# Expert order by place in the group, unpaced returned gathers and token-row gathers up to eight pairs ahead, in a macaron MoE and linear-attention block

## The reference

```python
logits = x @ gate_weight.T                      # 32 experts = 8 groups of 4
scores = softmax(logits)
group_scores = scores.reshape(T, 8, 4).max(axis=-1)
_, group_idx = top_k(group_scores, 3)           # 3 groups of 8
tmp_scores = where(expert is in one of these groups, scores, 0.0)
topk_weight, topk_idx = top_k(tmp_scores, 6)    # 6 experts of the 12
topk_weight = topk_weight / (topk_weight.sum() + 1e-20)
combine = zeros((T, E)).at[token, topk_idx].add(topk_weight)
for each expert e:
    y += combine[:, e] * ((silu(x @ w1[e].T) * (x @ w3[e].T)) @ w2[e].T)
y += (silu(x @ sw1.T) * (x @ sw3.T)) @ sw2.T    # the shared expert
```

## Time and profile before

| what | value |
|---|---|
| median of 3 runs | 855.51 us |
| the runs | 852.6, 855.51 and 856.67 us |
| span of the profiled execution, first to last instruction | 856.4 us |
| its own device time | not listed apart from the runs above |
| mean granted TensorE clock | 0.913 of full speed |
| layer 1, attention, layer 2 with its shared expert | about 0 to 296, 296 to 490, 490 to 856 us |
| loop of layer 2 | about 556 to 766 us |

### The profile page before, as it was taken

How to read it: one execution, slowest core, us unless ns; L and a number is a source line. 1 busy time by engine, 2 the same in 40 slices (tenths; PEclk the granted TensorE clock), 3 DMA queues, 4 the chain that set the end, 5 groups by cost and what they waited for, 6 DMA issues and landing times. The chain is left out here.

```text
span 856.4 us, 16278 instructions
## 1 busy us (share of the span) xinstructions
PE 734.5 (86%) x4554; PEld 590.7 (69%) x4555; DVE 515.1 (60%) x1439; ACT 361.0 (42%) x799; POOL 468.9 (55%) x487
## 2 busy tenths in 40 slices
PE   5888999999999987999999582799999999998900
PEld 5556788888888645777777481578888888874600
DVE  5685864444422568999997459977444442246652
ACT  2261444444455314556665231534444455531100
POOL 4003755555346455888864340275555637678784
PEclk9987999999999999999999755589999999999955
DMA  6792466744336552222232042144444435582234
GB/s 216 287 380 88 129 251 221 258 153 159 142 134 215 205 197 87 81 75 77 87 92 82 1 139 95 29 124 156 154 158 173 154 134 191 187 291 81 86 99 147
DMA packets 43591, 128.80 MB, mean 150 GB/s; under 512 B 8432, under 2 KB 16784, under 8 KB 40720
## 3 DMA queue, kind: packets, MB, share of 16 engines
q1 hardware_dynamic: 25104, 77.76, 24.1%
q0 software_dynamic: 18432, 50.36, 19.7%
HBM read 78.80 MB, written 49.28 MB: 150 GB/s over the span
## 5 line engine op out<-in xcount | busy, mean ns | idle before, releaser
L405 POOL DMA_INDIRECT back<-token_table,slots x192 | 186.2, 970 | 208.6 <-DVE slots L658 96.8
L930 PE MATMUL bank<-w,xt 128*128 x1024 | 244.7, 382 | 1.0 <-issue 0.6
L930 PEld LDWEIGHTS bank<-w,xt 128*128 128x128 f32 x1024 | 188.3, 192 | 24.7 <-issue 2.5
L706 DVE TENSOR_TENSOR mids<-mids,bank 128x256 f32<-128x256 f32 x128 | 53.7, 420 | 180.5 <-ACT mids L481 180.5
L950 PE MATMUL bank<-w,mids 128*128 x512 | 132.7, 382 | 0.1
L432 POOL DMA_INDIRECT back<-slot_table,combine x76 | 80.2, 1055 | 53.5 <-PE bank L930 25.1
L504 ACT COPY xt<-ring 128x256 f32 x256 | 91.2, 407 | 42.2 <-DVE ring L696 42.2
L950 PEld LDWEIGHTS bank<-w,mids 128*128 128x128 f32 x512 | 87.4, 190 | 9.1 <-issue 2.2
L481 ACT ACTIVATE mids<-bank 128x256 f32<-128x256 f32 x128 | 49.1, 384 | 102.3 <-PE bank L930 99.9
L696 DVE COPY ring<-bank 128x512 f32 (+1 forms) x96 | 66.3, 691 | 37.8 <-PE bank L920 37.0
L201 POOL DMA_INDIRECT ring<-slot_table,combine x64 | 65.4, 1021 | 27.1 <-issue 17.4
(11 more groups left out here) (208 smaller groups left out, 1096.5 us busy)
## 6 DMA issues: line engine op xcount, KB each, us to landing
slot_table<-gT SPq DMA_DIRECT2D x32, 512.0 KB
slot_table<-ey SPq DMA_DIRECT2D x32, 512.0 KB
w<-in_w SPq DMA_DIRECT2D x12, 1024.0 KB, 17.1
slot_table<-w SPq DMA_DIRECT2D x6, 1024.0 KB
token_table<-back SPq DMA_DIRECT2D x8, 512.0 KB, 2.9
back<-token_table,slots POOLq DMA_INDIRECT x192, 2.8
x<-in_x SPq DMA_DIRECT2D x4, 512.0 KB, 6.1
turn_a<-in_turn SPq DMA_DIRECT2D x4, 512.0 KB, 3.6
```

The costliest lines, as they stand in the source:

```text
L405: pool.indirect_dma_start(out=rows[q % RX][:, a * H:(a + 1) * H], out_offset=None, in_=table, in_offset=bass.IndirectOffsetOnAxis(ap=slots ...
L706: nc.vector.tensor_tensor(two(eg[u % 2][:, :]), two(es[u % 2][:, :]), part(u, 1), ALU.mult).then_inc(e_g, 1)
L930: last = nc.tensor.matmul(bH[u % 2][:, a * 2 * I:(a + 1) * 2 * I], xt[u % 2][:, a * H + k * P:a * H + (k + 1) * P], w13[:, bass.ds(expert[ ...
```

## The change

It has four parts. The columns of the mask, the exponentials and the weight arrays go by the place of an expert in its group: the first experts of the eight groups, then the second ones, and so on (`by_place` on the chip, `placed` on the host). The returned gathers of layer 2 no longer wait for `e_h`; those of layer 1 wait as before. The token-row gathers of layer 2 may be eight pairs ahead of the transposes, instead of four; layer 1 keeps four.

```diff
-AHEAD = 4
+AHEAD = 4, 8
-PACED = NQ - NT, NQ - 20
+PACED = NQ - NT
...
-                            if q >= AHEAD:
-                                pool.wait_ge(e_xp, read + q - AHEAD + 1)
+                            if q >= AHEAD[f]:
+                                pool.wait_ge(e_xp, read + q - AHEAD[f] + 1)
...
-                                if g % 2 == 0 and PACED[f] + g // 2 <= NQ:
-                                    pool.wait_ge(e_h, done + PACED[f] + g // 2)
+                                if f == 0 and g % 2 == 0 and PACED + g // 2 <= NQ:
+                                    pool.wait_ge(e_h, PACED + g // 2)
...
+                        def by_place(ap):
+
+                            return ap.rearrange("p (t e g) -> p t g e", g=NG, e=EG)
...
-                        nc.vector.tensor_scalar(v3(msk16[:, :], E), v3(val_out, PADE)[:, :, 0:E], 3e38, None, ALU.is_equal
-                                                ).then_inc(s_chosen, 1)
+                        nc.vector.tensor_scalar(by_place(msk16[:, :]), v3(val_out, PADE)[:, :, 0:E].rearrange(
+                            "p t (g e) -> p t g e", e=EG), 3e38, None, ALU.is_equal).then_inc(s_chosen, 1)
...
-                        nc.vector.tensor_tensor(v3(equal[:, :], E), v3(lg, E), wide(red[:, :], E), ALU.subtract
-                                                ).then_inc(s_d, 1)
+                        nc.vector.tensor_tensor(by_place(equal[:, :]), by_group(lg), red[:, :].unsqueeze(2).unsqueeze(3)
+                                                .broadcast_to([P, NT, NG, EG]), ALU.subtract).then_inc(s_d, 1)
...
+    def placed(m):
+
+        return m.reshape(NG, EG, *m.shape[1:]).swapaxes(0, 1).reshape(m.shape)
+
-    w13 = np.stack([a["w1"], a["w3"]]).reshape(2, NG, EG, I, KC, P).transpose(5, 1, 2, 4, 0, 3)
+    w13 = np.stack([placed(a["w1"]), placed(a["w3"])]).reshape(2, NG, EG, I, KC, P).transpose(5, 1, 2, 4, 0, 3)
...
-        "w2": a["w2"].transpose(2, 0, 1).reshape(I, -1),
+        "w2": placed(a["w2"]).transpose(2, 0, 1).reshape(I, -1),
```

## The result

The changed kernel takes 854.78 us at the median of 20 runs, against 857.15 us for the kernel before in 20 runs of the same comparison. The ratio is 0.9972, with a 95% interval of 0.9959 to 0.9985: faster by 0.28%, and so within the 0.5% called no change above. Forecast were 850.5 us, 0.6% faster. The range held the time; the size of the step was wrong. Two of the 20 runs of the changed kernel took 1485.85 and 2088.17 us and are not in the ratio; without them its median is 854.66 us.

A forecast was written before the change was run, and what follows sets the result against it. The kernel's end was taken as g46's start, plus 50 gathers, plus what VectorE's runs of adds cost them. 856.4 - 3.8 (gathers) - 1.5 (loop's end) + 0.3 (mask) = 851.4, stated as 850.5 us; range 847.0 to 855.5.

The forecast's parts named there:

- The pace: Layer 2's returned gathers, no longer waiting for TensorE, start g46 with the first add; gain three gathers, 3.8 us.
- The three limits on the gathers: Layer 2, g0 to g45: stores allow g0 at 688.0, last token-row gather near 684.6, buffers; g45 near 753.
- the idle time of 10 us: GpSimd in layer 2, after g45 near 753: idle some 10 us until VectorE's first add frees a buffer.
- the one long gather in the first run: In VectorE's first run of adds behind layer 2's loop, g48 is held up and takes over 3 us.
- The loop's end: End of layer 2's loop: the store lands 2.6 us earlier, at 759.8, so ScalarE stops waiting; gain 1.5 us.
- The mask: Strided write of the mask (L582), on the path in each layer: costs 0 to 0.5 us, taken as 0.3.
- The sum: Whole kernel: 856.4 - 3.8 - 1.5 + 0.3 = 851.4; stated as 850.5 us, the median lying 0.9 below the span.
- the main case: Whole kernel: gathers, loop's end and mask as summed, 850.5 us, own range 849.0 to 852.3; chance 0.47.
- (b): First run of adds behind the loop lets gathers through, 2.2 us more gain: 848.3 us; chance 0.13.
- (a): Loop's end stays as it was, only the gathers gain: 852.0 us; chance 0.2.
- (c): Nothing gets through the first run of adds, unpaced gathers bring nothing, only the loop's end gains: 854.3 us; chance 0.12.
- (d): Slower: faster gathers hold up stores between 741 and 762 us; store landing at 771 gives 860 us; chance 0.08.

The follow-up runs named there:

- a3: Changed kernel with mask, exponentials and weights back in the old group-by-group order of experts; 852.82 us, ratio 0.9961 to the kernel before.
- c2: Kernel before with only the pace (wait for `e_h`) of layer 2's returned gathers taken away, old order and four pairs of lead; ratio 0.9956.
- c1: Changed kernel with the pace of 44 + g/2 put back for layer 2's returned gathers, new order and eight pairs of lead kept; ratio 1.0001.
- b1: a2 with `KEEP = 24`, so 42 buffers for returned rows instead of 46; ratio 0.9984 to the kernel before.
- c3: a2 with column 0 and half of column 1 added inside the loop, and the store of pairs 56 and 57 ahead of the four loads; 841.8 us, 0.9811.
- a1: Changed kernel run again unaltered; 853.15 us against 855.86 for the kernel before, ratio 0.9953.
- a4: Kernel before with the order of experts by place alone, paced and four pairs of lead; 856.16 us, ratio 0.9988.
- a2: Changed kernel with the mask and `equal` lines reading with the stride and writing in a row; ratio 0.9949 to the kernel before.

## Why the prediction was right or wrong

**The pace: right, in place and size.** Forecast were three gathers, 3.8 us. B without long gathers is 80.5 to 80.6 in the three paced profiles and 76.2 to 77.0 in the five unpaced ones with 46 buffers and whole adds behind the loop: 3.5 to 4.4. The three limits on the gathers (stores, GpSimd's own order, buffers), the idle time of 10 us and the one long gather in the first run stand in the profile as forecast. That order and lead give nothing at g46 is shown by a3 and c2, and from the other side by c1.

**The loop's end: right in mechanism, too large in size.** I took 1.5 us and counted the store as early enough; 0.9 was measured. It landed near 760.65 (751.17 + 9.48), in a loop that ran 0.73 us ahead of the one before; on the clock of the profile before that is 761.4, where 759.8 was worked out and 760.9 would have been early enough. A fell by 1.07 in this profile and, by the means of the two profiles of the changed kernel (3.6) and of the three paced ones (4.5), by 0.9. The step assumed that the queue of the loads and stores drains at the common rate once the gathers are gone. A follows when the gathers end: 2.82 when they end at 749 (b1), 3.3 to 4.0 at 753, 4.3 to 5.0 when they run on. Beside the loads that are queued ahead of the store (c3), the few gathers up to 753 still cost something, and the estimate gave them nothing.

**The mask: this is the step that failed.** The term was "between 0 and 0.5 us, and I take 0.3", bounded above by the row of L585. By the rows it is 0.86 us in each layer (1.28 to 1.31 against 0.43), 1.7 in all. In layer 2 the path shows it: from its first transposes to its first `up` it is 65.67 to 65.85 us in the four profiles with the strided write (changed, a1, a4, c1) and 64.85 to 64.98 in the three with the old one (before, a3, c2). In layer 1 it doesn't stand out: from the mask's start to the first `up` it is 46.7 to 49.1 us in those four and 48.2 to 48.3 in those three. The bound was no bound: I took a row with as many elements, but written in a row, as the price of a strided write, and L585 itself became slower under its stride, 1.06 against 0.69. No row of before showed a strided write of this kind. The Trainium skill (VectorE: DVE Perf Modes, section What auto-detection actually checks) gave 0 as I read it; the trace says otherwise, and the measurement decides. Reading with the stride costs 0.18 to 0.19 us (a2).

**The sum.** With the forecast's 3.8 for the pace, which its 3.5 to 4.4 holds, and with what was measured for the others it is -3.8 - 0.9 + 1.7 = -3.0 us, -0.35%. The measured ratio is 0.9972 (0.9959 to 0.9985), a1 has 0.9953 (0.9932 to 0.9973), and -0.35% lies within both. The forecast was -5.0. Of the 4.3 us between 850.5 and 854.78, 1.6 are the median before (857.15 instead of 855.51), 1.4 the masks and 0.6 the loop's end; the remaining 0.7 is less than the runs spread. The same terms give 0.9956 for c2 (0.9956 measured), 0.9949 for a2 (0.9949), 0.9956 for a3 (0.9961) and 1.0020 for c1 (1.0001, with 1.0020 as the end of its interval). For a4 they give 1.0020 as well, and there they fail (0.9988, at most 1.0007). So the part of the masks rests on the rows and not on the times.

Two slips in the prediction's own figures changed no term. The bounds of the mask and the store (0 to 0.5 and 0 to 1.5) give the main case 850.2 to 852.2 us, and not 849.0 to 852.3, so less of it was below 851.2 than the two thirds that the chance of "faster" counts. And the profile before has a long gather in four of its five runs of adds, not three.

**The rivals.** (b) happened in a2, whose adds and gathers are those of the changed kernel. It is less a rival than a throw of each execution: of the nine profiles with all adds behind the loop and two SBUF operands (before, changed, a1 to a4, b1, c1, c2) the first run has a long gather in eight, the second in seven. One more or less is 1.9 to 3.9 us in these nine, as much as the whole change. (a) happened in part: the loop's end kept 0.6 of its 1.5 us. (c) and (d) did not happen. The time stands near the 854.3 us of (c), but by chance: two gathers got through the first run and the unpaced gathers did bring their 3.8 us. The store was never as late as (d) needs. That the range held the time is luck in part too, since most of the masks' cost and the higher median before were in none of its terms.

**What stays open.** Why one gather of a run of adds is held up until its end, and why in some executions none is, at the same distance from the run's start to 0.01 us. The other spread, ahead of layer 2, was not tested either. In layer 1 the granted clock fell at different times; the rows give busy times, granted clock, DMA share and GB/s, before and then after (columns: the stretch and its length, busy time and number of instructions of PE, PEld, DVE, ACT and POOL, then the clock, the DMA share and GB/s):

```profile
38.00:45.00 7.00, 2.43 (x32) 1.74 (x32) 6.48 (x31) 2.42 (x4) 0.00 (x0) 1.00 1.01 427
45.00:54.00 9.00, 8.85 (x18) 3.83 (x19) 7.31 (x31) 3.89 (x4) 0.00 (x0) 0.81 1.01 421
...
66.00:84.00 18.00, 14.09 (x65) 11.75 (x64) 11.84 (x48) 2.61 (x3) 6.24 (x7) 0.71 0.18 61
```

```profile
38.00:45.00 7.00, 4.45 (x33) 2.46 (x32) 6.48 (x28) 3.00 (x4) 0.00 (x0) 0.76 1.01 427
45.00:54.00 9.00, 8.12 (x25) 4.18 (x26) 8.04 (x32) 3.55 (x4) 0.00 (x0) 1.00 1.01 422
...
66.00:84.00 18.00, 14.09 (x74) 11.86 (x71) 12.66 (x50) 2.61 (x3) 7.88 (x8) 0.81 0.22 71
```

A clock of 1.00 is the level of 2.4 GHz, and the means between mix it with 1.2. Before, the clock was down in part of the stretch from 45 to 54 us, after in part of that from 38 to 45, and from 66 to 84 it was up for longer. The first `up` of layer 1 started at 87.25 before and 85.60 after although the mask came 0.8 us later, and in a1, the same kernel, it started at 87.16.

## What to carry to other kernels

When a later stage is bound by a queue of transfers, count how many of them are left when the first buffer comes free, and price the change in whole transfers: here 1.27 us each, checked by taking four buffers away. If buffers are the limit, free them earlier instead of filling them faster; the adds moved into the loop took the ratio to 0.979, where the kernels without the pace alone stand at 0.995 to 0.997. And price a reordering by a row with the same stride on the same side; here reading with the stride and writing in a row was the cheaper form.

## What the runs showed of the hardware that was not expected

- A write of 128x512 in float16 with a stride of 8 elements took VectorE 1.28 to 1.31 us from float32 in SBUF, against 0.43 us in a row and 0.61 to 0.62 us with the stride on the reading side. In float32 from PSUM it was 1.06 against 0.69 us, and 0.69 with the strided read.
- In runs of VectorE's adds with two SBUF operands a gather of GpSimd takes up to 8.01 us instead of 0.96, until about 0.8 us behind the run's end. With one operand in PSUM, at the same density, none took over 1 us in two runs of one profile.
- A store of 512 KB behind 2 MB of loads, with gathers beside it, kept ScalarE waiting 2.4 to 4.2 us. Ahead of the loads, with the gathers, it did not (one profile); behind them, with the gathers gone, the wait was 1.3 us and cost TensorE nothing (one profile).
